# A fused attention, mixture and attention network: an earlier split of expert weights through PSUM, and loads in finer pieces

## The chip, the cores and the metric

One core of a Trainium2 chip runs the whole program. The metric is the device time of one execution in microseconds, the median of several; less is better. Times in the trace are microseconds from the first instruction.

The engines are TensorE (PE; PEld is its loading of weights), VectorE (DVE), ScalarE (ACT), GpSimd (POOL) and SyncE (SP). Each works its own list of instructions in order, and they wait for each other by semaphores.

## What is computed

Four layers on `x` of 8 x 512 tokens with 128 channels, each behind a layer norm and added to `x`: a recurrent attention, a mixture of 8 experts, a second recurrent attention with an MLP, and a mixture of 16 experts. The change lies at the end of the first layer and around the second:

```python
logits = jax.nn.relu(x @ rw1 + rb1) @ rw2 + rb2
vals, ids = jax.lax.top_k(logits, K)                    # K = 2 of E = 8
probs = jax.nn.softmax(vals, axis=-1)
...
pos = jnp.cumsum(m, axis=0) - 1                         # place of a token in its expert
keep = (pos_tok < CAP).astype(x.dtype)                  # CAP = 512
disp = jnp.zeros((E, CAP, Cx), x.dtype).at[ids_f, pos_c].add(xr * keep[:, None])
h = jax.nn.relu(jnp.einsum('enc,ech->enh', disp, ew1) + eb1[:, None, :])
eo = jnp.einsum('enh,ehc->enc', h, ew2) + eb2[:, None, :]
y = eo[ids_f, pos_c] * (probs_f * keep)[:, None]
return y.reshape(Bx, Tx, K, Cx).sum(axis=2)
```

## The kernel before

The program runs in stages, split by barriers: at `stage_end(eng, k)` an engine adds to `stage_done` and waits until all four compute engines have; GpSimd only adds to it, and SyncE takes no part. B = 8 batches of 512 tokens, each NT = 4 tiles of 128.

**Stage 5** ends the first attention and routes the tokens. It is one pipeline over the batches, written out by hand on each engine. In iteration b TensorE makes the router's hidden layer (`router_hidden`), the transposed logits (`router_logits_T`), the transposed tokens of the next batch (`transpose5`), the variance of the attention's output two batches on (`variance_o`, four matmuls with one column) and the logits by token (`router_logits`). ScalarE applies relu, copies the transposed tokens as float16 (`xT5_copy`) and takes square roots (`deviation_o` waits for the variance). VectorE makes the low half of the tokens (`xT5_low`, L1405), picks the two largest logits (`route`), turns counts into slots of `disp` (`place_picks`, whose last line L1438 signals `slots`), and adds the attention's output two batches on.

GpSimd copies rows of tokens to `disp` in DRAM: `scatter(b)` issues eight indirect DMAs (L635), one for each tile and choice, 64 in all. It waits for the slots of batch b, and at the third tile, ahead of the fifth DMA, for the logits of batch b + 1 (in the last batch for `s_eb2_mm`, the experts' output bias spread over the partitions by TensorE).

Products of 32-bit values are made of float16 halves: the high half of a value w is w * 1024 rounded to float16, the low half is what is left, and three matmuls (`PARTS`) replace one. For the 8 experts `weights0_high(k)` (ScalarE, L890) and `weights0_low(k)` (VectorE, L1472) make the halves of 1024 columns, k = 0 to 3 for the first layer and 4 to 7 for the second. Six of the eight are made at the end of stage 5, two inside stage 6. The float16 halves lie in A2 and A3, where the rows to be scattered lie before them, so the high halves wait for the scatters of batches 0 to 3 (`s_scattered[0]`) and 4 to 6 (`s_scattered[1]`).

At its end TensorE runs `unread` passes, matmuls of 512 columns whose result nobody reads, 20 ahead of the barrier and 18 behind it. VectorE copies the spread bias (`eb2_rep`, L1466), makes the low halves, and then the coefficients of the two experts from ScalarE's Exp (L1479 to L1483). SyncE waits until all scatters have landed and loads `disp` into `xd` by four DMAs of two experts each (L498).

**Stage 6** runs the experts: `transpose_rows(e)`, float16 halves on ScalarE (L904) and VectorE (L1489), `hidden0(e)` and `outputs0(e)` on TensorE. GpSimd scatters the outputs to `y_rows` in DRAM.

**Behind it** SyncE loads `y_rows` back, two DMAs of 256 KB for each batch (L507, one for each choice). `combine(b)` on VectorE (L1537) adds both choices to `resid` by eight multiply-adds, four for each choice, and then makes the statistics of the next layer norm. These loads lie in the same tiles (A6, A7) as the experts' weights before.

PSUM has 8 banks of 512 columns. In stage 5 banks 0 to 3 carry the attention's centred output, the transposed tokens and the router's hidden layer, bank 4 the projection, bank 5 the transposed logits, 6 the logits and counts, 7 the variances; 6 and 7 then the spread bias.

## Time and profile before

| | us |
|---|---|
| median of 3 runs | 928.3 (927.37 to 928.76) |
| the profiled execution | 927.65 |
| its span, first to last instruction | 925.6 |
| mean granted TensorE clock | 0.962 |

```profile
## 1 busy us (share of the span) xinstructions
PE 774.7 (84%) x6154; PEld 469.3 (51%) x6154; DVE 693.2 (75%) x2078; ACT 622.2 (67%) x932; POOL 632.3 (68%) x414
```

The 2.05 us between the span and the profiled execution's time lie outside the instructions. Stage 5 runs from about 208 to 323 us, the experts from 331 to 384, the return starts at 388. A record gives the start of an instruction, its duration, and in brackets how long its engine sat idle before it and what ended that. A row in which an operation carries xN merges N of them.

### The profile page before, as it was taken

The page shows a single profiled execution, that of the slowest core. Times are in us where ns is not written, and L with a number is a line of the kernel's source. Part 1 is how long each engine was busy: PE and PEld are TensorE (multiplying, and loading weights), DVE is VectorE, ACT ScalarE, POOL GpSimd, SP SyncE. Part 2 cuts the span into 40 slices and gives each one's busy share as a digit, 9 for nine tenths or more (in the row PEclk, how much of TensorE's full clock was granted, in tenths as well). Part 3 has the DMA queues.
Part 4 walks back from the last instruction along what each step waited for, and adds up shares of the span by engine and source line. Part 5 has one row for each costly group of instructions (what it writes and reads, how often), then busy time and mean ns, then how long its engine had stood idle before and what let it go on. Part 6 is the DMA issues. An engine that isn't in the chain of part 4 may idle for free.

```text
span 925.6 us, 18384 instructions
## 1 busy us (share of the span) xinstructions
PE 774.7 (84%) x6154; PEld 469.3 (51%) x6154; DVE 693.2 (75%) x2078; ACT 622.2 (67%) x932; POOL 632.3 (68%) x414
## 2 busy tenths in 40 slices
PE   4965765669998689468787989999999999999997
PEld 1343221224543357323233756767776777777775
DVE  7769899985777558498999878776666666666664
ACT  3755233323455367248778988888888888989895
POOL 4008899730577727558798997686868686868695
PEclk9987899899999899879999999999999999999999
DMA  5999300008200030252600000000000000000000
GB/s 150 118 120 202 115 0 0 18 3 211 69 21 7 3 101 26 68 149 58 204 1 1 1 1 2 13 1 11 0 11 0 8 4 0 11 0 11 0 13 13
DMA packets 52761, 40.47 MB, mean 44 GB/s; under 512 B 6028, under 2 KB 44703, under 8 KB 52703
## 3 DMA queue, kind: packets, MB, share of 16 engines
q1 hardware_dynamic: 49630, 37.28, 18.5%
q0 software_dynamic: 3072, 2.51, 0.9%
q8 instruction: 24, 0.39, 0.2%
q14 instruction: 35, 0.28, 0.1%
HBM read 18.07 MB, written 14.88 MB: 36 GB/s over the span
## 4 chain that ended last, share of the span: by engine, by line
POOL 24%; PE 18%; issue 14%; DVE 14%; ACT 6%; DMA 1%; POOLq 0%; DVEq 0%; ACTq 0%; SPq 0%
POOL scratch L725 20%; PE PS L1874 17%; DVE scratch L1635 2%; DVE resid L1537 2%; DVE stats L1375 1%; DVE scratch L1643 1%; POOL disp L635 1%; POOL resid L711 1%; PE PS L1881 1%; ACT scratch L1163 1%; ACT scratch L1159 1%; DVE resid L1388 1%; DVE A L1400 1%; DVE scratch L1378 1%; ACT A L1094 1%
## 5 line engine op out<-in xcount | busy, mean ns | idle before, releaser
L725 POOL TENSOR_TENSOR scratch<-scratch 128x1024 f16<-128x1024 f32 x128 | 273.0, 2135 | 84.5 <-ACT scratch L1163 82.3
L1822 DVE SCALAR_TENSOR_TENSOR resid<-PS,coef,resid 128x128 f32<-128x128 f32 x512 | 144.0, 344 | 108.8 <-PE PS L1874 103.4
L1874 PEld LDWEIGHTS PS<-A,scratch 128*128 128x128 f16 x3456 | 203.4, 98 | 37.9 <-POOL scratch L725 4.9
L1874 PE MATMUL PS<-A,scratch 128*128 128x128 f16 x3456 | 217.1, 219 | 3.9 <-POOL scratch L725 1.6
L1874 PE MATMUL PS<-A 128*128 (+1 forms) x768 | 186.8, 379 | 0.8 <-DVE A L1666 0.2
L1159 ACT ACTIVATE scratch<-PS,cols 128x512 f32<-128x512 f32 x256 | 163.9, 683 | 25.9 <-PE PS L1874 19.0
L1163 ACT ACTIVATE scratch<-scratch 128x1024 f16<-128x1024 f32 x128 | 135.3, 1057 | 5.0
L1874 PE MATMUL PS<-scratch,ident 128*128 128x512 f32 x160 | 89.4, 681 | 51.9 <-DVE scratch L1341 51.9
L594 POOL TENSOR_TENSOR scratch<-A 128x1024 f32<-128x1024 f32 x32 | 76.0, 2384 | 73.2 <-DVE A L1310 56.2
L1874 PEld LDWEIGHTS PS<-A 128*128 128x128 f16 x768 | 70.7, 98 | 66.6 <-issue 0.7
L635 POOL DMA_INDIRECT disp<-A,scratch x64 | 65.5, 1023 | 36.4 <-issue 30.0
L1874 PEld LDWEIGHTS PS<-scratch,ident 128*128 128x128 f32 x160 | 30.8, 210 | 100.0 <-DVE scratch L1341 77.7
L1332 DVE TENSOR_TENSOR_SCAN PS<-PS,scratch 128x512 f32<-128x512 f32 x64 | 74.9, 1216 | 1.9
L1874 PE MATMUL PS<-scratch,A 128*128 128x512 f16 (+1 forms) x216 | 52.5, 389 | 2.1 <-DVE scratch L1489 1.1
L652 POOL DMA_INDIRECT y_rows<-A x32 | 34.3, 1072 | 28.7 <-DVE A L1504 24.7
L1881 PE MATMUL PS<-ident,scratch 128*128 128x128 f32 x128 | 21.5, 294 | 36.7 <-ACT scratch L949 16.7
L674 POOL TENSOR_TENSOR scratch<-scratch,A 128x1024 f32<-128x1024 f32 x16 | 38.6, 2415 | 12.2 <-DVE scratch L1635 4.4
L1874 PE MATMUL PS<-scratch,w_r 128*8 128x512 f32 (+1 forms) x106 | 40.2, 509 | 5.9 <-DVE scratch L1718 3.0
L663 POOL TENSOR_SCALAR A<-resid,scratch 128x128 f32<-128x128 f32 x32 | 31.3, 988 | 19.6 <-DVE scratch L1549 19.6
L818 ACT ACTIVATE PS<-A 128x512 f32<-128x512 f32 x33 | 19.7, 599 | 35.8 <-DVE PS L1332 35.7
L818 ACT ACTIVATE PS<-scratch 128x512 f32<-128x512 f32 x31 | 18.6, 601 | 36.6 <-DVE PS L1332 36.0
L1635 DVE TENSOR_TENSOR_SCAN scratch<-PS,scratch 128x512 f32<-128x512 f32 x32 | 37.3, 1207 | 2.5 <-POOL scratch L674 1.2
(334 smaller groups left out, 1321.0 us busy)
## 6 DMA issues: line engine op xcount, KB each, us to landing
A<-A SPq DMA_DIRECT2D x22, 256.0 KB, 7.5
y_rows<-zeros SPq DMA_DIRECT2D x8, 512.0 KB, 6.0
A<-y_rows SPq DMA_DIRECT2D x16, 256.0 KB, 3.5
disp<-zeros SPq DMA_DIRECT2D x4, 528.0 KB, 21.6
A<-disp SPq DMA_DIRECT2D x4, 528.0 KB, 6.0
resid<-in_L_attn_x SPq DMA_DIRECT2D x8, 256.0 KB, 4.0
A<-scratch SPq DMA_DIRECT2D x8, 256.0 KB, 6.9
A<-in_L_ffn_ew SPq DMA_DIRECT2D x1, 2048.0 KB, 12.4
```

The costliest lines, as they stand in the source:

```text
L594: pool.tensor_tensor(c_ring[n % 3], bkR[:, 2 * p:2 * p + 2, :], vR[:, i, :].unsqueeze(1).to_broadcast([128, 2, T]), MUL).then_inc(S("r0_c" ...
L635: pool.indirect_dma_start(out=disp[:, :], in_=rows5[RING_OF[b]][:, k, t, :], in_offset=None, out_offset=bass.IndirectOffsetOnAxis(ap=slot_ ...
L652: pool.indirect_dma_start(out=y_rows[:, :], in_=eo[:, ex * NT + t, :], in_offset=None, out_offset=bass.IndirectOffsetOnAxis(ap=xd[:, ex * ...
L674: pool.tensor_tensor(cbuf[n % 2], cs[n % 2], v1[:, bts(b, T)].unsqueeze(1).to_broadcast([128, 2, T]), MUL).then_inc(S("r_c"), 1)
L725: pool.tensor_tensor(h_low[n % 4], h_full[n % 2], h_high[n % 4], SUB).then_inc(S("m1_low"), 1)
L818: A_(bank(n % 2), kk_pair(a, m)[:, max(i, j) % 2, :], ACT.Identity, scale=-1.0, bias=1.0).then_inc(S("r0_decay"), 1)
L1159: A_(h_full[e % 2][:, h * T:(h + 1) * T], bank((e * HC1 + h) % 4), ACT.Gelu, scale=1.0 / SCALE, bias=cols[:, MB1 + e * HC1 + h:MB1 + e * H ...
L1163: A_(h_high[e % 4], h_full[e % 2], ACT.Copy).then_inc(S("m1_high"), 1)
L1332: V.tensor_tensor_scan(out=bank(2 + 2 * (n % 2) + u), data0=bank(u), data1=c_ring[n % 3][:, u, :], initial=0.0, op0=MUL, op1=ADD).then_inc ...
L1635: last = V.tensor_tensor_scan(out=state[:, j, :], data0=bank(2 + j), data1=cbuf[n % 2][:, j, :], initial=0.0, op0=MUL, op1=ADD)
L1822: last = STT(out=resid[:, g, :], in0=bank(4 + e % 2)[:, t * C:(t + 1) * C], scalar=coef[b % 2][:, t, e:e + 1], in1=resid[:, g, :], op0=MUL ...
L1874: return nc.tensor.matmul(o, l, r, start=start, stop=stop)
```

## The change

Two changes are made together.

In stage 5 TensorE runs `variance_o(b + 2)` behind `router_logits(b)` and no longer ahead of it. GpSimd's wait for the logits of batch 1 moves from the third tile of batch 0 to the fourth. ScalarE makes the first three high halves at the ends of iterations 5, 6 and 7. It copies each of the first six high halves back, as 32-bit values, to PSUM (banks 0 and 1, or 2 and 3, in turn), and VectorE's low half reads it there. A copy waits for its own high half and, from the third on, for the low half two before it. Exp comes behind the third copy. VectorE copies `eb2_rep` behind the six low halves. The unread passes go to bank 4, 30 ahead of the barrier and 6 behind it.

The loads of `disp` are one expert, one expert, three and three. The return of batch 0 comes in halves of two tiles, four DMAs, counted by the semaphores of the `disp` loads; `combine(0)` works on each half when it is there. SyncE waits for landed loads from batch 3 on, no longer from batch 2.

On TensorE, from one iteration of stage 5 (transposes of the next batch, L1881 and L1916; logits, L2027 and L2062; `meancol` is the variance's operand), before:

```order
L1874 MATMUL PS<-scratch,w_r 8x512 x4
L1881 MATMUL PS<-ident,A 128x128 x4
L1874 MATMUL PS<-meancol,scratch 128x1 x4
L2027 MATMUL PS<-ident,scratch 128x8 x4
L1874 MATMUL PS<-w_q,scratch 128x128 x4
```

and now:

```order
L1909 MATMUL PS<-scratch,w_r 8x512 x4
L1916 MATMUL PS<-ident,A 128x128 x4
L2062 MATMUL PS<-ident,scratch 128x8 x4
L1909 MATMUL PS<-meancol,scratch 128x1 x4
L1909 MATMUL PS<-w_q,scratch 128x128 x4
```

The logits stand ahead of the variance; nothing else moved there. On ScalarE, from iteration 7 of stage 5 to the first expert (relu L857, logits L863, high halves L890, transposed rows L904), before:

```order
L857 ACTIVATE scratch<-PS,cols 128x512 x4
L863 ACTIVATE scratch<-PS 8x512
L893 ACT_TABLE_LOAD
L893 ACTIVATE tmpb<-tmpa 128x32
L890 ACTIVATE A<-A 128x2x512 x6
L904 ACTIVATE scratch<-PS 128x512 x2
```

and now, from the second early high half in the iteration before (L894 high halves, L901 copies to PSUM, L926 Exp):

```order
L894 ACTIVATE A<-A 128x2x512
L877 ACTIVATE scratch<-PS,cols 128x512 x4
L883 ACTIVATE scratch<-PS 8x512
L894 ACTIVATE A<-A 128x2x512
L901 ACTIVATE PS<-A 128x1024 x3
L926 ACT_TABLE_LOAD
L926 ACTIVATE tmpb<-tmpa 128x32
L894 ACTIVATE A<-A 128x2x512
L901 ACTIVATE PS<-A 128x1024
L894 ACTIVATE A<-A 128x2x512
L901 ACTIVATE PS<-A 128x1024
```

Two high halves moved into the rounds, the third ahead of Exp, six copies are new, and the table load stands behind three of them. On VectorE, behind the last batch's routing, before:

```order
L1464 TENSOR_TENSOR tmpa<-scratch 128x32
L1466 COPY A<-PS 128x1024
L1475 TENSOR_TENSOR w_r<-pickg 128x512
L1472 SCALAR_TENSOR_TENSOR A<-A 128x2x512 x6
L1479 TENSOR_SCALAR tmpa<-tmpb 128x32
```

and now:

```order
L1496 TENSOR_TENSOR tmpa<-scratch 128x32
L1504 TENSOR_TENSOR w_r<-pickg 128x512
L1501 SCALAR_TENSOR_TENSOR A<-A,PS 128x2x512 x6
L1508 COPY A<-PS 128x1024
L1510 TENSOR_SCALAR tmpa<-tmpb 128x32
```

The copy of the bias moved behind the low halves, which now read A and PSUM instead of A twice.

The diff:

```diff
--- before.py
+++ after.py
@@ -381,7 +381,20 @@
         e0_hl1 = A2[:, :].bitcast(f16).rearrange("p (e s n) -> p e s n", e=E0, s=2)
         e0_hl2 = A3[:, :].bitcast(f16).rearrange("p (e s n) -> p e s n", e=E0, s=2)
         E0_SPLITS = 2
+        EARLY, BESIDE = 3, 6
+
+        def high_made(k):
+            return at(E0_SPLITS + (k if k < EARLY else 2 * k if k < BESIDE else k + BESIDE))
+
+        def beside_made(k):
+            return at(E0_SPLITS + (EARLY + k if k < EARLY else 2 * k + 1))
+
+        def high_at(k):
+            return bank(k % 2 * 2, 2)
+
         PARTS = ((0, 0), (0, 1), (1, 0))
+        XD_PARTS = ((0, 1), (1, 2), (2, 5), (5, E0))
+        XD_PART_OF = (0, 1, 2, 2, 2, 3, 3, 3)
 
         r7 = carve(7)[:, 688:688 + 2 * TILES].rearrange("p (s n) -> p s n", s=2)
         nm7 = carve(7)[:, 752:752 + TILES]
@@ -494,15 +507,22 @@
             sp.wait_ge(s_scattered[1], 16 * TOP0 * NT * (B - 5))
             sp.wait_ge(s_scattered[2], 16 * TOP0 * NT)
             dv = disp.rearrange("(n p) c -> p n c", p=128)
-            for k in range(E0 // 2):
-                sp.dma_start(xd[:, bts(k, 2 * NT), :], dv[:, bts(k, 2 * NT), :]).then_inc(s_disp[k], 16)
+            for k, (low, high) in enumerate(XD_PARTS):
+                part = slice(low * NT, high * NT)
+                sp.dma_start(xd[:, part, :], dv[:, part, :]).then_inc(s_disp[k], 16)
 
             sp.wait_ge(s_eo, 16 * E0 * NT)
             sp.wait_ge(S("split_low"), at(E0_SPLITS + 7))
             yv = y_rows.rearrange("(k n p) c -> k p n c", k=TOP0, p=128)
             for b in range(B):
-                if b >= 2:
-                    sp.wait_ge(s_fetched[b % 2], X_LOADS + 16 * TOP0 * (b // 2))
+                if b == 0:
+                    for half in range(2):
+                        for k in range(TOP0):
+                            part = slice(half * NT // 2, (half + 1) * NT // 2)
+                            sp.dma_start(fetched[k][:, part, :], yv[k][:, part, :]).then_inc(s_disp[half], 16)
+                    continue
+                if b >= 3:
+                    sp.wait_ge(s_fetched[b % 2], X_LOADS + 16 * TOP0 * ((b - 1) // 2))
                 for k in range(TOP0):
                     sp.dma_start(fetched[k][:, bts(b, NT), :], yv[k][:, bts(b, NT), :]).then_inc(s_fetched[b % 2], 16)
 
@@ -626,9 +646,9 @@
                 pool.wait_ge(S("rows5"), at(b))
                 pool.wait_ge(S("ids5"), at(b))
                 for t in range(NT):
-                    if t == NT // 2 and b + 1 < B:
+                    if t == (NT // 2 if b else NT - 1) and b + 1 < B:
                         pool.wait_ge(S("lg5_mm"), at(b + 1))
-                    elif t == NT // 2:
+                    elif t == NT // 2 and b + 1 == B:
                         pool.wait_ge(s_eb2_mm, 1)
                     for k in range(TOP0):
                         g = b * NT + t
@@ -868,6 +888,18 @@
             deviation_x5(0)
             deviation_o(1)
             xT5_copy(0)
+            def weights0_high(k):
+                hl, w = ((e0_hl1, e0w1), (e0_hl2, e0w2.rearrange("p e i c -> p e (i c)")))[k // 4]
+                two = slice(2 * (k % 4), 2 * (k % 4) + 2)
+                A_(hl[:, two, 0, :], w[:, two, :], ACT.Copy, scale=SCALE).then_inc(S("split_high"), 1)
+
+            def weights0_beside(k):
+                hl = (e0_hl1, e0_hl2)[k // 4]
+                if k >= 2:
+                    act.wait_ge(S("split_low"), at(E0_SPLITS + k - 2))
+                act.wait_ge(S("split_high"), high_made(k))
+                A_(high_at(k), hl[:, 2 * (k % 4):2 * (k % 4) + 2, 0, :], ACT.Copy).then_inc(S("split_high"), 1)
+
             for b in range(B):
                 for h in range(HC0):
                     relu5(b, h)
@@ -884,18 +916,18 @@
                     square_o(2)
                 elif b + 2 < B:
                     deviation_o(b + 2)
-            def weights0_high(k):
-                hl, w = ((e0_hl1, e0w1), (e0_hl2, e0w2.rearrange("p e i c -> p e (i c)")))[k // 4]
-                two = slice(2 * (k % 4), 2 * (k % 4) + 2)
-                A_(hl[:, two, 0, :], w[:, two, :], ACT.Copy, scale=SCALE).then_inc(S("split_high"), 1)
-
+                if b >= B - EARLY:
+                    act.wait_ge(s_wm, 32)
+                    act.wait_ge(s_scattered[0], 16 * TOP0 * NT * 4)
+                    weights0_high(b - B + EARLY)
+            for k in range(EARLY):
+                weights0_beside(k)
             act.wait_ge(S("lg_less"), at(0))
             A_(tmpb[:, :], tmpa[:, :], ACT.Exp).then_inc(S("lg_exp"), 1)
-            act.wait_ge(s_wm, 32)
-            act.wait_ge(s_scattered[0], 16 * TOP0 * NT * 4)
             act.wait_ge(s_scattered[1], 16 * TOP0 * NT * (B - 5))
-            for k in range(6):
+            for k in range(EARLY, BESIDE):
                 weights0_high(k)
+                weights0_beside(k)
             stage_end(act, 5)
 
 
@@ -1462,19 +1494,18 @@
                 if b + 2 < B:
                     add_o(b + 2)
             TT(tmpa[:, :], top0[:, 1, :], top0[:, 0, :], SUB).then_inc(S("lg_less"), 1)
-            dve.wait_ge(s_eb2_mm, 1)
-            st.done(V.tensor_copy(eb2_rep, bank(6, 2).rearrange("p k (e c) -> p (k e) c", c=C)))
-
             def weights0_low(k):
                 hl, w = ((e0_hl1, e0w1), (e0_hl2, e0w2.rearrange("p e i c -> p e (i c)")))[k // 4]
                 two = slice(2 * (k % 4), 2 * (k % 4) + 2)
-                dve.wait_ge(S("split_high"), at(E0_SPLITS + k))
-                STT(out=hl[:, two, 1, :], in0=w[:, two, :], scalar=SCALE, in1=hl[:, two, 0, :],
+                dve.wait_ge(S("split_high"), beside_made(k) if k < BESIDE else high_made(k))
+                STT(out=hl[:, two, 1, :], in0=w[:, two, :], scalar=SCALE, in1=high_at(k) if k < BESIDE else hl[:, two, 0, :],
                     op0=MUL, op1=SUB).then_inc(S("split_low"), 1)
 
             TT(pick2, pickg[:, 0], pickg[:, 1], ADD)
-            for k in range(6):
+            for k in range(BESIDE):
                 weights0_low(k)
+            dve.wait_ge(s_eb2_mm, 1)
+            st.done(V.tensor_copy(eb2_rep, bank(6, 2).rearrange("p k (e c) -> p (k e) c", c=C)))
             dve.wait_ge(S("lg_exp"), at(0))
             st.done(TS(tmpa[:, :], tmpb[:, :], 1.0, None, ADD))
             st.done(V.reciprocal(tmpa[:, :], tmpa[:, :]))
@@ -1530,14 +1561,18 @@
 
 
             def combine(b):
-                dve.wait_ge(s_fetched[b % 2], X_LOADS + 16 * TOP0 * (b // 2 + 1))
-                for k in range(TOP0):
-                    for t in range(NT):
-                        g = b * NT + t
-                        last = STT(out=resid[:, g, :], in0=fetched[k][:, g, :], scalar=coef0[:, k, g:g + 1],
-                                   in1=resid[:, g, :], op0=MUL, op1=ADD)
-                    if k < TOP0 - 1:
-                        links.done(last)
+                if b:
+                    dve.wait_ge(s_fetched[b % 2], X_LOADS + 16 * TOP0 * ((b + 1) // 2))
+                for part in ((0, 1), (2, 3)) if b == 0 else (range(NT),):
+                    if b == 0:
+                        dve.wait_ge(s_disp[part[0] // 2], BACK[part[0] // 2] + 16 + 16 * TOP0)
+                    for k in range(TOP0):
+                        for t in part:
+                            g = b * NT + t
+                            last = STT(out=resid[:, g, :], in0=fetched[k][:, g, :], scalar=coef0[:, k, g:g + 1],
+                                       in1=resid[:, g, :], op0=MUL, op1=ADD)
+                        if k < TOP0 - 1:
+                            links.done(last)
                 last.then_inc(S("moe_added"), 1)
                 dve.wait_ge(S("moe_added"), at(b))
                 token_stats(b).then_inc(S("x_var"), 1)
@@ -1590,7 +1625,7 @@
                 dve.wait_ge(S("gate_high"), at(m))
                 TT(gate_hl[:, 1, c], whole_gate(m), gate_hl[:, 0, c], SUB).then_inc(S("gate_low"), 1)
 
-            dve.wait_ge(S("split_high"), at(E0_SPLITS + 8))
+            dve.wait_ge(S("split_high"), high_made(8))
             for low, w, high in ((u1_hl[:, 1, :], u_1[:, :], u1_hl[:, 0, :]), (u2_hl[1], u_2[:, :, :], u2_hl[0]),
                                  (ur_hl[:, 1, :], u_r[:, :], ur_hl[:, 0, :])):
                 STT(out=low, in0=w, scalar=SCALE, in1=high, op0=MUL, op1=SUB)
@@ -2052,9 +2087,9 @@
                 router_logits_T(b)
                 if b + 1 < B:
                     transpose5(b + 1)
+                router_logits(b)
                 if b and b + 2 < B:
                     variance_o(b + 2)
-                router_logits(b)
                 if b == 0:
                     centre(2)
                     unread(3, 4)
@@ -2067,13 +2102,13 @@
             for e in range(E0):
                 last = mm(tile(bank(6 + e // 4), e % 4), spread[:, e, :], eb2[:, :])
             last.then_inc(s_eb2_mm, 1)
-            unread(3, 20)
+            unread(4, 30)
             stage_end(pe, 5)
-            unread(3, 18)
+            unread(4, 6)
 
 
             def transpose_rows(e):
-                pe.wait_ge(s_disp[e // 2], BACK[e // 2] + 16)
+                pe.wait_ge(s_disp[XD_PART_OF[e]], BACK[XD_PART_OF[e]] + 16)
                 pe.wait_ge(S("xdT"), at(e, 2))
                 transposes(bank(e % 2), xd[:, bts(e, NT), 0:C]).then_inc(S("trd"), 1)
```

## Rows read from the trace of the kernel before

**Rows 1.** Chain of waits, 320 to 330 us: start, us, what.
```profile
323.24 2.11 DMA disp<-A,scratch
325.43 4.01 DMA A<-disp
```
**Rows 2.** GpSimd's timeline, stage 5: start, us, what, [idle before <-releaser].
```profile
244.04 0.97 POOL L635 DMA_INDIRECT disp<-A,scratch  x1 [3.93 <-PE PS L2027]
...
286.10 0.97 POOL L635 DMA_INDIRECT disp<-A,scratch  x1 [0.50 <-issue]
...
301.53 0.97 POOL L635 DMA_INDIRECT disp<-A,scratch  x1 [0.30 <-issue]
...
306.65 0.97 POOL L635 DMA_INDIRECT disp<-A,scratch  x1 [0.30 <-issue]
...
315.60 1.52 POOL L635 DMA_INDIRECT disp<-A,scratch  x1 [0.31 <-issue]
317.42 1.97 POOL L635 DMA_INDIRECT disp<-A,scratch  x1 [0.30 <-issue]
319.69 1.96 POOL L635 DMA_INDIRECT disp<-A,scratch  x1 [0.30 <-issue]
```
**Rows 3.** TensorE's timeline: variance, logits, unread passes, first expert.
```profile
284.02 0.95 PE L1874 MATMUL PS<-meancol,scratch 128*128 128x1 f32 x8
284.90 0.41 PE L2027 MATMUL PS<-ident,scratch 8*128 8x8 f32 x4
...
304.85 0.41 PE L2027 MATMUL PS<-ident,scratch 8*128 8x8 f32 x4 [0.68 <-ACT scratch L863]
...
313.35 5.81 PE L1874 MATMUL PS<-pickg,ones 128*128 128x512 f16 x20
323.07 5.64 PE L1874 MATMUL PS<-pickg,ones 128*128 128x512 f16 x18 [3.91 <-DVEq L181]
...
331.68 5.63 PE L1874 MATMUL PS<-scratch,A 128*128 128x512 f16 x24 [1.11 <-DVE scratch L1489]
```
**Rows 4.** VectorE's timeline, 299 to 323 us.
```profile
299.90 0.16 DVE L1438 TENSOR_TENSOR scratch<-scratch 128x8 int32<-128x8 f32 x1
...
309.44 0.18 DVE L1464 TENSOR_TENSOR tmpa<-scratch 128x32 f32<-128x32 f32 x1
313.45 1.22 DVE L1466 COPY A<-PS 128x1024 f32<-128x1024 f32 x1 [3.83 <-PE PS L1874]
...
315.05 6.89 DVE L1472 SCALAR_TENSOR_TENSOR A<-A 128x1024 f16<-128x1024 f32 x6
...
322.80 0.18 DVE L1483 TENSOR_TENSOR scratch<-scratch,tmpb 128x32 f32<-128x32 f32 x1
```
**Rows 5.** ScalarE's timeline, 297 to 319 us.
```profile
297.03 1.33 ACT L857 ACTIVATE scratch<-PS,cols 128x512 f32<-128x512 f32 x2 [1.18 <-PE PS L1874]
...
304.81 1.28 ACT L893 ACT_TABLE_LOAD   x1
...
313.23 5.79 ACT L890 ACTIVATE A<-A 128x1024 f16<-128x1024 f32 x6 [3.35 <-DMA disp<-A,scratch]
```
**Rows 6.** TensorE by windows: window, length, PE busy (count), clock, DMA share, GB/s.
```profile
323.00:324.00 1.00, 0.93 (x3) 0.50 0.02 1
...
406.00:408.00 2.00, 0.73 (x2) 1.00 0.56 162
```
**Rows 7.** The return: timelines of SyncE and VectorE, line L507, a smaller load.
```profile
388.47 16.12 SPq L507 DMA_DIRECT2D A<-y_rows  x16
...
392.40 2.31 DVE L1537 SCALAR_TENSOR_TENSOR resid<-A,scratch,resid 128x128 f32<-128x128 f32 x8 [8.18 <-DMA A<-y_rows]
...
L507 SPq DMA_DIRECT2D A<-y_rows x16: 359/508/515, 388.5 to 404.1; - x16
...
DMA to landing us min/median/max: 2.9/3.5/4.6
...
A<-scratch SPq DMA_DIRECT2D x32, 64.0 KB, 2.0
```

## What the change was predicted to do

> **What bounds the kernel now.** First the chain of waits over 300 to 340 us [rows 1]. The last of 64 scatters of tokens to `disp` starts at 323.24; 2.11 us later SyncE issues the loads of `disp` (325.43), the first lands 4.01 us later (329.44), and after transposes, ScalarE's high half and VectorE's low half TensorE starts on the experts' first matmuls at 331.68 [rows 3], 2.24 us behind the landing. From there TensorE is the bound of the mixture, so what is gained before it moves everything behind it. The barrier of the stage opens at 323.07 [rows 3], 6.4 us before the landing: it isn't late now.
>
> Second, GpSimd's timeline [rows 2]. The scatters go at one per 1.28 us (0.97 busy, 0.30 between). They wait once in each batch of eight for the router's logits of the next batch: with logits at 284.90 + 0.41 = 285.31 [rows 3] the scatter behind the wait starts at 286.10, 0.79 later, and that row has 0.50 idle instead of 0.30. So each wait costs 0.2 us, and 0.79 is the least distance between release and start. Then three scatters are stretched, to 1.52, 1.97 and 1.96 us. They lie inside the six low halves of the weights on VectorE, 315.05 to 321.94 [rows 4], whose two inputs are both in SBUF; the scatters beside VectorE's copy from PSUM at 313.45 and beside ScalarE's high halves [rows 5] keep their pace.
>
> Last, the return from the mixture [rows 7]: SyncE issues at 388.47, VectorE starts at 392.40 after 8.18 us idle and needs 2.31 for eight multiply-adds. Everything later waits for that.
>
> **The change part by part.**
>
> *The low halves read the high half from PSUM.* If the second SBUF input is what stretches the scatters, this gives back 0.55 + 1.00 + 0.99 = 2.54 us (1.52, 1.97, 1.96 against 0.97) [rows 2]. Nothing in the trace shows a scatter beside such an operation with one input in PSUM; the nearest row is the copy from PSUM at 313.45, which stretched none. Bounds 0 and 2.54, I take 2.54. The rule of the Trainium skill bears on it both ways (SBUF — State Buffer, "Who interferes with whom"): two SBUF inputs hold a port pair shared with GpSimd, one does not; but it adds, marked as inferred, that such an operation takes only the read side, while making descriptors needs the write side. By the first the sum keeps its 2.54, by the second the stretching had another cause and would stay, which is rival 1.
>
> *Variance behind the logits, and the first batch's wait moved by two scatters.* The four small matmuls of a variance take 0.88 us of TensorE ahead of the logits (284.02 to 284.90 [rows 3]); the logits come that much earlier in iterations 1 to 5. VectorE's routing doesn't start earlier, since it is still busy with the low half of the transposed tokens when the logits are there. GpSimd saves its 0.2 us a batch. In the first batch two more scatters go ahead of the wait of 3.93 us [rows 2]. Neither can bring more than the next limits allow: the scatters of a batch wait for its slots (batch 6: 299.90 + 0.16 = 300.06 [rows 4], first scatter 301.53, so 301.53 − 300.06 − 0.79 = 0.68 us of slack), and the logits of batch 7, which have no variance ahead of them, come at 304.85 + 0.41 = 305.26 against a scatter at 306.65: 306.65 − 305.26 − 0.79 = 0.60 us. So the scatters gain 0.60 (bounds 0.4 and 0.7). The variance's later reader on ScalarE slips 0.2 us and has over a microsecond of idle behind it.
>
> Together the last scatter and the load's issue move by 3.14: issue at 325.43 − 3.14 = 322.29.
>
> *Finer loads of `disp`.* Expert 0 alone is 264 KB. Loads of 256 KB land in 2.9 (shortest) to 3.5 us (median) [rows 7], two experts took 4.01. I take 3.2; expert 1, issued under 0.9 later, lands at about 4.0 as now, and its transposes (0.5) hide in the 2.24 us that expert 0 needs to its first matmul. First matmul by this path: 322.29 + 3.2 + 2.24 = 327.73, against 331.68: **3.95 us** earlier (3.1 if expert 0 lands no earlier than both now).
>
> *The barrier, which hid and may now bind.* ScalarE's first two early high halves (six in a row take 5.79, 0.97 each; one alone, whose end nothing hides, I take as 1.05) fit in idle time of its rounds, the tightest 1.18 us [rows 5]. After its last router copy (304.80): third high half to 305.8, copies to PSUM 0 and 1 to 307.8 (no row shows such a copy; 1024 columns from SBUF took 1.05, I take the same, bound 1.2). VectorE is through its routing at 309.62, `pick2` to 310.0, lows 0 and 1 at 1.15 each to 312.3; ScalarE's third copy waits for low 0 and ends at 312.3; then the table load for Exp, which now lies open (1.28), and Exp (0.23): 313.8. Then three times high half, wait for itself, copy: 1.08 + 0.97 = 2.05 each, the last copy ending at 320.1; low 5 to 321.35; `eb2_rep`, moved behind, 1.22; the five small operations that take 321.87 to 322.98 now, 1.11. Sum: barrier at about 323.75, 0.7 later than now. A matmul of 512 columns costs 0.235 us at the full clock (24 in 5.63 at 331.68 [rows 3]). The 20 unread passes from 313.35, 5.81 us, become 30, 5.81 + 10 × 0.235 = 8.16, to 321.5; TensorE is idle 2.2 us; six passes after the barrier take 1.4, to 325.15. Expert 0's rows land at 325.5. So the barrier is hidden by 0.3 us, and each further microsecond of it costs one. If ScalarE's copies take 1.2, it comes 0.5 later and costs 0.2.
>
> *The clock.* Granted clock was 0.50 of full (1.2 of 2.4 GHz) in 323 to 324, after 3.91 us idle, and stayed 1.00 in 406 to 408, with 0.73 of 2 us busy [rows 6]. Idle of 2.2 us lies between the two; I take it to stay up, with the other case as rival 2.
>
> *Return in halves.* A first half needs two loads of 128 KB. 64 KB landed in 2.0, 256 KB in 2.9 to 3.5 [rows 7]; I take 2.5. Issues cost 0.51 each: second load at 388.98, landed 391.5; four multiply-adds to 392.75; the second half, issued to 390.0, landed 392.5, done at 394.05 against 392.40 + 2.31 = 394.71: **0.65 us** (0 if 128 KB take as long as 256; 1.3 with 2.0). The loads of batch 1 are issued 1 us later but are needed at 397.
>
> *The rest.* Six more copies on ScalarE are counted above; the eighth and seventh weight splits keep both inputs in SBUF, inside the mixture, where TensorE binds. Different banks for the unread passes cost nothing.
>
> **Sum.** 3.95 + 0.65 = 4.6 us off the profiled execution of 927.65 gives 923.05; off the median of 928.3, 0.65 above it, **923.7**. What separates from no change is 0.2%, 1.86 us, so 926.44.
>
> **Rivals.**
>
> 1. *The scatters stay stretched* (the cause is not the second SBUF input). Three lows now end by 313.5 and three run from 316 to 321.4, beside the last scatters, so about the same 2.54 us are lost again. Issue 324.83, first matmul 330.27, gain 1.4 + 0.65 = 2.05: **926.2**. For: nothing shows the mixed form. Against: the stretch begins and ends with the lows.
>
> 2. *The barrier and the clock bind.* The clock falls in the idle time before the barrier: six passes at half of it, 0.47, take 2.8, transposes start at 326.55, and with the transposes' own slowness (0.4) the first matmul comes at 329.2. The 18 passes behind the barrier now took 5.64 us [rows 3] against 18 × 0.235 = 4.23: 1.4 us is what the lower clock costs until it rises, and that would fall on the experts' matmuls. Gain 331.68 − 329.2 − 1.4 = 1.1, plus 0.65: **926.5**. For: the drop after 3.91 us idle and only six passes instead of 18 behind the barrier. Against: the idle time is shorter by 1.7 us.
>
> 3. *Slower: the scatters, moved against VectorE's rounds by 0.6 us, hold up its SBUF-only operations.* A round is 10.5 us and VectorE's chain bounds it. If a scatter held up the chain by its own 0.97 us in each of seven rounds, that is 6.8 us, against 4.6 gained: **930.5**. It turns slower than no change beyond 0.66 us a round. Against: now scatters cover three quarters of each round, so most phases are tried already, and rounds don't vary.
>
> 4. *Finer loads bring nothing*, neither for `disp` nor in the return: 3.1 + 0 = 3.1: **925.2**, still faster.
>
> **How the numbers follow.** Forecast with its small variations (922.4 to 924.7) 0.56; rival 4 and cases between 0.10; rival 1 0.10, of which half below 926.44; rival 2 0.17, of which 0.06 faster; rival 3 0.05; other losses 0.02. Faster: 0.56 + 0.10 + 0.05 + 0.06 = 0.77. Same: 0.05 + 0.11 + 0.01 = 0.17. Slower: 0.05 + 0.01 = 0.06. The range reaches from 922.3 (both bounds of the small gains) to 926.9, past rivals 1 and 2; about 0.1 lies outside above and less below.
>
> **What would show it.** In the changed profile: all scatters from the 57th on at 0.97, else the first step is wrong; the last scatter starts near 320.1; the load of `disp` is issued near 322.3 and lands first near 325.5; the barrier opens near 323.75 (later than 324.2: my count of ScalarE's pairs is wrong, and TensorE's start is read from the barrier instead); the granted clock is 1.00 behind it; first expert matmul near 327.7; rounds still 10.5 us; 16 returns, then VectorE's eighth multiply-add of batch 0 ends 0.65 us sooner after SyncE's issue. From the first expert matmul to SyncE's return issue should stay 56.8 us; if not, something moved inside the mixture that I have not seen.

## The result and the profile after

| | before | after |
|---|---|---|
| median of 6 runs | 927.84 us (927.0 to 928.91) | 924.11 us (922.24 to 925.51) |
| profiled execution, its span | 927.65, 925.6 | 925.51, 923.3 |
| mean granted TensorE clock | 0.962 | 0.953 |

The ratio is 0.9958, 95% interval 0.9947 to 0.9968: 3.7 us faster, where 4.6 was forecast (923.7, range 922.3 to 926.9). The profiled execution was forecast at 923.05 and took 925.51.

The profiled execution after is the slowest of its six. Its stages 1 to 3, which the change doesn't touch, took 2.0 us longer, so absolute times of the two traces can't be set side by side. TensorE's granted clock was lower there: 0.77 against 0.89 over 45 to 75 us, 0.83 against 0.90 over 100 to 150 us. I count all times of stage 5 and of the experts from the first unread pass of stage 5: 208.33 before, 210.35 after. "At 112.21" below means 112.21 us after that pass.

| us after the first unread pass of stage 5 | before | after | forecast gain | gain |
|---|---|---|---|---|
| last scatter starts | 114.91 | 112.21 | 3.14 | 2.70 |
| SyncE issues the loads of `disp` | 117.10 | 114.39 | 3.14 | 2.71 |
| first rows landed, behind the issue | 4.01 | 2.98 | 0.8 | 1.03 |
| first expert matmul | 123.35 | 119.61 | 3.95 | 3.74 |
| from there to the issue of the return | 56.79 | 56.75 | 0 | 0.04 |
| from that issue to batch 0's last multiply-add | 6.24 | 5.55 | 0.65 | 0.69 |

(The third row is a duration from the issue in the row above it; the last two are durations too.)

The chain of waits of the kernel after (start, us, what) against [rows 1]:

```profile
322.56 2.11 DMA disp<-A,scratch
324.74 2.98 DMA A<-disp
...
327.76 0.67 PE PS L1916 x4
```

GpSimd's timeline after, against [rows 2]. The scatters from the 57th on (at 313.62) all take 0.97. The waits in the middle of the batches have not gone: GpSimd sits idle 0.62 to 0.69 us there in batches 1 to 5, where it was 0.50 or less before, and only in batch 6 (308.49) nothing more than the usual 0.30:

```profile
287.63 0.97 POOL L655 DMA_INDIRECT disp<-A,scratch  x1 [0.69 <-issue]
...
298.27 0.97 POOL L655 DMA_INDIRECT disp<-A,scratch  x1 [0.62 <-issue]
...
308.49 0.97 POOL L655 DMA_INDIRECT disp<-A,scratch  x1 [0.31 <-issue]
...
317.45 0.97 POOL L655 DMA_INDIRECT disp<-A,scratch  x1 [0.31 <-issue]
318.72 0.97 POOL L655 DMA_INDIRECT disp<-A,scratch  x1 [0.30 <-issue]
320.00 0.97 POOL L655 DMA_INDIRECT disp<-A,scratch  x1 [0.30 <-issue]
```

TensorE after, against [rows 3]: logits of batch 7, 30 passes, then the barrier (2.29 idle), six passes, and the transposes right behind them, released by the rows' landing with 0.20 idle:

```profile
307.30 0.41 PE L2062 MATMUL PS<-ident,scratch 8*128 8x8 f32 x4 [0.68 <-ACT scratch L883]
...
315.86 7.94 PE L1909 MATMUL PS<-pickg,ones 128*128 128x512 f16 x30
326.08 1.47 PE L1909 MATMUL PS<-pickg,ones 128*128 128x512 f16 x6 [2.29 <-DVEq L181]
327.76 0.66 PE L1916 MATMUL PS<-ident,A 128*128 128x128 f32 x4 [0.20 <-DMA A<-disp]
...
329.96 5.63 PE L1909 MATMUL PS<-scratch,A 128*128 128x512 f16 x24 [0.67 <-DVE scratch L1520]
```

VectorE after, against [rows 4]: low halves waiting for ScalarE's copies, the bias copy behind them, the last coefficient 0.09 us ahead of the barrier's opening:

```profile
312.39 3.52 DVE L1501 SCALAR_TENSOR_TENSOR A<-A,PS 128x1024 f16<-128x1024 f32 x3
318.30 1.22 DVE L1501 SCALAR_TENSOR_TENSOR A<-A,PS 128x1024 f16<-128x1024 f32 x1 [2.38 <-ACT PS L901]
320.39 1.22 DVE L1501 SCALAR_TENSOR_TENSOR A<-A,PS 128x1024 f16<-128x1024 f32 x1 [0.88 <-ACT PS L901]
322.49 1.22 DVE L1501 SCALAR_TENSOR_TENSOR A<-A,PS 128x1024 f16<-128x1024 f32 x1 [0.88 <-ACT PS L901]
323.63 1.22 DVE L1508 COPY A<-PS 128x1024 f32<-128x1024 f32 x1
...
325.81 0.18 DVE L1514 TENSOR_TENSOR scratch<-scratch,tmpb 128x32 f32<-128x32 f32 x1
```

The return after (VectorE), against [rows 7]: two groups of four multiply-adds. SyncE's first issue is at 386.71.

```profile
389.44 1.26 DVE L1572 SCALAR_TENSOR_TENSOR resid<-A,scratch,resid 128x128 f32<-128x128 f32 x4 [6.98 <-DMA A<-y_rows]
391.00 1.26 DVE L1572 SCALAR_TENSOR_TENSOR resid<-A,scratch,resid 128x128 f32<-128x128 f32 x4 [0.30 <-DMA A<-y_rows]
```

### The profile page after: what moved, and what is told of

The parts are those of the page before. It is cut to its first block, busy times and chain, and to the rows that moved or that the text cites. A ratio compares the mean times of both kernels' runs of the same rounds, so it can differ in the third digit from the quotient of the medians.

```text
span 923.3 us, 18395 instructions
## 1 busy us (share of the span) xinstructions
PE 779.5 (84%) x6152; PEld 471.9 (51%) x6152; DVE 693.6 (75%) x2078; ACT 628.5 (68%) x938; POOL 628.3 (68%) x414
## 4 chain that ended last, share of the span: by engine, by line
POOL 24%; PE 19%; DVE 14%; issue 14%; ACT 6%; DMA 1%; POOLq 0%; SPq 0%; DVEq 0%; ACTq 0%
POOL scratch L745 21%; PE PS L1909 18%; DVE scratch L1670 2%; DVE resid L1572 2%; DVE stats L1407 1%; DVE scratch L1678 1%; POOL resid L731 1%; PE PS L1916 1%; DVE resid L1420 1%; ACT scratch L1195 1%; ACT scratch L1191 1%; DVE A L1432 1%; DVE scratch L1410 1%; ACT A L1126 1%; POOL scratch L694 1%
## 5 line engine op out<-in xcount | busy, mean ns | idle before, releaser
L655 POOL DMA_INDIRECT disp<-A,scratch x64 | 62.5, 977 | 36.9 <-issue 32.7
L1916 PE MATMUL PS<-ident,scratch 128*128 128x128 f32 x128 | 21.5, 295 | 36.2 <-ACT scratch L981 16.0
```

What stands on the lines that cost most here:

```text
L655: pool.indirect_dma_start(out=disp[:, :], in_=rows5[RING_OF[b]][:, k, t, :], in_offset=None, out_offset=bass.IndirectOffsetOnAxis(ap=slot_ ...
```

## Experiments

All are variants of the changed kernel. The ratios are to the kernel before on the same chip: it took 927.84 us beside the changed kernel, 927.46 beside e1 to e4, and 928.74 beside e7, e5b, e6b and e8b. So small differences between medians of different sets are better read from the ratios. The last two columns are from one trace each, in us after the first unread pass of stage 5.

| kernel | median us | ratio, 95% interval | last scatter | first expert matmul |
|---|---|---|---|---|
| changed | 924.11 | 0.9958 (0.9947 to 0.9968) | 112.21 | 119.61 |
| e1_low_from_sbuf | 927.54 | 0.9999 (0.9989 to 1.0010) | 115.85 | 123.21 |
| e2_no_early | 930.60 | 1.0037 (1.0025 to 1.0050) | 112.25 | 126.27 |
| e3_disp_by_two | 924.91 | 0.9968 (0.9957 to 0.9980) | 112.26 | 120.72 |
| e4_return_whole | 923.74 | 0.9963 (0.9949 to 0.9977) | 112.28 | 119.62 |
| e7_passes_18 | 927.37 | 0.9988 (0.9977 to 0.9999) | 112.23 | 121.80 |
| e5b_order_back | 924.20 | 0.9956 (0.9939 to 0.9974) | 112.36 | 119.68 |
| e6b_variance_back | 923.08 | 0.9945 (0.9925 to 0.9965) | 112.41 | 119.60 |
| e8b_tail_behind | 923.94 | 0.9946 (0.9929 to 0.9963) | 112.35 | 119.83 |

### The second SBUF input

```diff
-STT(out=hl[:, two, 1, :], in0=w[:, two, :], scalar=SCALE, in1=high_at(k) if k < BESIDE else hl[:, two, 0, :],
+STT(out=hl[:, two, 1, :], in0=w[:, two, :], scalar=SCALE, in1=hl[:, two, 0, :],
```

> The changed kernel, but the low halves read the high half from SBUF again, as before; ScalarE still makes the copies to PSUM, and VectorE still waits for them, so nothing but the place of one input differs. Times are counted from the first unread pass of stage 5, where before and after start alike: the last scatter starts at 114.91 us before the change and at 112.21 behind it. Theory (the second SBUF input stretches the scatters): scatters beside the six low halves last 1.5 to 2.0 instead of 0.97, the last one starts 2 to 5 us later than 112.21, the experts' first matmul (119.61 behind the change) follows it, and the median is 2 to 4 us above the changed kernel's 924.1. Rival (the stretching came from something else, such as the traffic of that moment or the descriptors' writing): the scatters keep 0.97 and the time stays within 1 us of the changed kernel's.

GpSimd's timeline of e1_low_from_sbuf:

```profile
313.67 1.97 POOL L655 DMA_INDIRECT disp<-A,scratch  x1 [0.30 <-issue]
315.94 0.97 POOL L655 DMA_INDIRECT disp<-A,scratch  x1 [0.30 <-issue]
317.22 0.97 POOL L655 DMA_INDIRECT disp<-A,scratch  x1 [0.30 <-issue]
318.50 1.94 POOL L655 DMA_INDIRECT disp<-A,scratch  x1 [0.30 <-issue]
320.74 1.79 POOL L655 DMA_INDIRECT disp<-A,scratch  x1 [0.30 <-issue]
322.83 1.79 POOL L655 DMA_INDIRECT disp<-A,scratch  x1 [0.30 <-issue]
324.92 0.97 POOL L655 DMA_INDIRECT disp<-A,scratch  x1 [0.30 <-issue]
```

and VectorE's, its low halves:

```profile
312.44 3.53 DVE L1501 SCALAR_TENSOR_TENSOR A<-A 128x1024 f16<-128x1024 f32 x3
318.36 1.23 DVE L1501 SCALAR_TENSOR_TENSOR A<-A 128x1024 f16<-128x1024 f32 x1 [2.38 <-ACT PS L901]
320.45 1.23 DVE L1501 SCALAR_TENSOR_TENSOR A<-A 128x1024 f16<-128x1024 f32 x1 [0.87 <-ACT PS L901]
322.55 1.22 DVE L1501 SCALAR_TENSOR_TENSOR A<-A 128x1024 f16<-128x1024 f32 x1 [0.87 <-ACT PS L901]
```

Only the place of one input differs, and four scatters are stretched again: 1.97, 1.94, 1.79 and 1.79, together 3.6 us, as much as the last scatter comes later (115.85 against 112.21). The last three long ones each lie across one low half (318.36, 320.45, 322.55), and the two scatters in VectorE's pause between 315.97 and 318.36 keep 0.97. The low half itself takes 1.22 us either way. The rival is refuted, and the time is back at that of the kernel before. Of the rules of the Trainium skill that the prediction weighed (SBUF — State Buffer, "Who interferes with whom"), the first, that two SBUF inputs contend with GpSimd and one does not, agrees with this trace (1.79 to 1.97 us here beside two inputs in SBUF, 0.97 in the changed kernel beside one); the remark marked there as inferred, which would have spared the scatters, does not. Which step inside a scatter is held up no run shows.

This experiment shows a second thing. TensorE is idle 2.23 us before the barrier, makes its six passes in 1.47, waits 3.64 us for the rows, and the granted clock falls afterwards. TensorE's timeline and windows (length, busy and count, clock, DMA share, GB/s) of e1_low_from_sbuf:

```profile
331.26 0.66 PE L1916 MATMUL PS<-ident,A 128*128 128x128 f32 x4 [3.64 <-DMA A<-disp]
...
333.56 6.45 PE L1909 MATMUL PS<-scratch,A 128*128 128x512 f16 x24
```
```profile
328.00:331.00 3.00, 0.00 (x0) 1.00 0.48 129
331.00:334.00 3.00, 2.00 (x10) 0.73 1.01 256
334.00:337.00 3.00, 3.00 (x11) 0.70 1.09 300
```

The first 24 matmuls take 6.45 instead of 5.63 us, and the experts as a whole 57.41 instead of 56.75.

### The early high halves and the barrier

```diff
-        EARLY, BESIDE = 3, 6
+        EARLY, BESIDE = 0, 6
...
+            act.wait_ge(s_wm, 32)
+            act.wait_ge(s_scattered[0], 16 * TOP0 * NT * 4)
```

> The changed kernel with no early high halves: all six high halves and all six copies to PSUM come behind the scatters of batch 6, as the high halves did before. Theory (the barrier is bound by ScalarE's pairs at 2.05 us each and VectorE's tail of 2.3 us behind the last low half): six pairs take 12.3 us from about 315.0 on the clock of the changed kernel's profile, the barrier opens near 330.8 instead of 326.08, the experts' first matmul comes 4 to 5 us later than 119.61 us after the first unread pass of stage 5, and the median is near 928.5, no better than the kernel before. Rival (the barrier has slack, the loads of disp bind): the first matmul moves by less than 1 us and the median stays near 924.

TensorE's timeline of e2_no_early:

```profile
329.62 2.74 PE L1911 MATMUL PS<-pickg,ones 128*128 128x512 f16 x6 [6.13 <-DVEq L181]
332.16 1.65 PE L1918 MATMUL PS<-ident,A 128*128 128x128 f32 x8
334.76 1.47 PE L1911 MATMUL PS<-scratch,A 128*128 128x512 f16 x6 [0.96 <-DVE scratch L1522]
```

The barrier opens at 121.13 instead of 115.73 (5.40 later, 4.7 expected), the six passes take 2.74 instead of 1.47, with a granted clock of 0.50, that is 1.2 of 2.4 GHz, over 329 to 333 us, and the first matmul comes 6.66 later (126.27). The median is 930.6, 6.5 above the changed kernel and 3.1 above the kernel before. The mechanism is the expected one; its size was missed by some 2 us. 0.7 of it is the barrier's own delay, 1.27 the six passes at the lower clock, which I had not charged; from their end to the first matmul it takes 2.40 us against 2.41, so the transposes add nothing more. Reading from PSUM without the early high halves is thus slower than the kernel before.

### The pieces of the loads

```diff
-        XD_PARTS = ((0, 1), (1, 2), (2, 5), (5, E0))
-        XD_PART_OF = (0, 1, 2, 2, 2, 3, 3, 3)
+        XD_PARTS = ((0, 2), (2, 4), (4, 6), (6, E0))
+        XD_PART_OF = (0, 0, 1, 1, 2, 2, 3, 3)
```

> The changed kernel with the loads of disp two experts each again. Theory (finer loads give the difference between 4.0 us for two experts and 3.0 for one): the first landing is 4.0 us behind SyncE's issue instead of 2.98, the experts' first matmul comes 0.8 to 1.0 us later than 119.61, the median is 925.0. Rival (the second expert's rows, not the first's, release the first matmul, so that the finer loads bring nothing): no change within 0.2 us.

The chain of waits of e3_disp_by_two:

```profile
322.75 2.11 DMA disp<-A,scratch
324.93 4.03 DMA A<-disp
329.01 0.67 PE PS L1916 x4
```

4.03 us to the first landing against 2.98, and the first matmul at 120.72, 1.11 later than 119.61. The second expert's rows do not bind in the changed kernel: its transposes start at 118.28, 1.3 us ahead of the first matmul. The median is 0.8 us higher and the ratios are 0.9968 and 0.9958; their intervals overlap. The gain is shown by the trace, not by the medians.

### The return in halves

```diff
-                    for half in range(2):
-                        for k in range(TOP0):
-                            part = slice(half * NT // 2, (half + 1) * NT // 2)
-                            sp.dma_start(fetched[k][:, part, :], yv[k][:, part, :]).then_inc(s_disp[half], 16)
+                    for k in range(TOP0):
+                        sp.dma_start(fetched[k][:, 0:NT, :], yv[k][:, 0:NT, :]).then_inc(s_disp[0], 16)
...
-                for part in ((0, 1), (2, 3)) if b == 0 else (range(NT),):
+                for part in (range(NT),):
```

> The changed kernel with batch 0 returned in two whole loads and combined at once, as before; the looser waits of the later batches stay. Theory: from SyncE's first issue of the return to the end of batch 0's eighth multiply-add it takes 6.24 us again instead of 5.55, and the median is 0.7 us above the changed kernel's 924.1, 924.8. Rival (part of the 0.69 us is chance of one execution or due to the looser waits): the stretch stays under 5.9 us.

SyncE's and VectorE's timelines of e4_return_whole:

```profile
385.29 0.91 SPq L520 DMA_DIRECT2D A<-y_rows  x2
```
```profile
389.00 2.31 DVE L1570 SCALAR_TENSOR_TENSOR resid<-A,scratch,resid 128x128 f32<-128x128 f32 x8 [7.96 <-DMA A<-y_rows]
```

From issue to the end of the eighth multiply-add: 3.71 + 2.31 = 6.02 us. With halves it was 5.55 in the changed kernel's profile and between 5.0 and 5.6 in those of e1, e2, e3, e5b, e6b, e7 and e8b, which return in halves too. So by these traces halves are worth 0.4 to 1.0 us, and some 0.2 of the difference to 6.24 before is chance or the looser waits of the later batches. The measured 6.02 lies between what theory (6.24) and rival (under 5.9) expected. It is one trace against eight, and a first run of e8 (below), with halves, took 5.86; so the size stays rough. The medians of e4 and the changed kernel (923.74 and 924.11) don't show it: it is smaller than their intervals.

### The passes behind the barrier

```diff
-            unread(4, 6)
+            unread(4, 18)
```

> The changed kernel with 18 unread passes behind the barrier, as before the change, instead of 6; nothing else differs. Theory (once the loads land early, passes behind the barrier stand in the way of the transposes): passes start 115.73 us after the first unread pass of stage 5 and take 4.2 to 4.6 us, the transposes start near 120.1 instead of 117.41, the experts' first matmul comes 2.5 us later than 119.61, the median is 2.5 us above the changed kernel's. Rival (the barrier or the loads bind, passes are free): less than 0.5 us.

TensorE's timeline of e7_passes_18:

```profile
324.26 4.06 PE L1909 MATMUL PS<-pickg,ones 128*128 128x512 f16 x18 [1.06 <-DVEq L181]
328.16 1.04 PE L1916 MATMUL PS<-ident,A 128*128 128x128 f32 x8
330.30 4.06 PE L1909 MATMUL PS<-scratch,A 128*128 128x512 f16 x18 [1.11 <-DVE scratch L1520]
```

The passes end at 119.8, the transposes start at 119.66, 2.25 later than in the changed kernel, and the first matmul comes at 121.80, 2.19 later (2.5 expected). Passes that hid behind the loads before [rows 3] are in the way once the loads land early. The median is 3.3 us above the changed kernel's (2.8 by the ratios), of which the trace explains 2.2; the rest stays open.

### The order of stage 5

```diff
-                    if t == (NT // 2 if b else NT - 1) and b + 1 < B:
+                    if t == NT // 2 and b + 1 < B:
...
-                router_logits(b)
                 if b and b + 2 < B:
                     variance_o(b + 2)
+                router_logits(b)
```

e6 has the second edit alone. Both were run first on a chip on which the kernel before took 951.0 us; they were run again on another.

> The changed kernel with the variance ahead of the logits again and the first batch's wait at the third tile: the order of stage 5 is that of before. In the changed kernel the rounds lost 0.43 us in sum, VectorE's four normalising operations taking 1.15 to 1.22 instead of 1.12 in several rounds. Theory (the scatters, moved earlier, now overlap these operations and hold them up; the scatters gained 0.60 from earlier releases and lost 0.43 by the longer rounds): these operations take 1.12 again, rounds are 10.51 us, and the last scatter comes 0.17 us later than 112.21, the median within 0.3 of the changed kernel's. Rival (the longer rounds come from the new ScalarE work in iterations 5 and 6 or from nothing in the order): rounds stay longer and the last scatter comes 0.6 later.

> The changed kernel with only the variance ahead of the logits again; the first batch still has two more scatters ahead of its wait. Theory (the earlier logits are what lets the scatters run ahead in every round, the moved wait only helps in the first batch): scatters start ahead by 0.7 us in batch 1 and lose it again by about 0.2 us a round, the waits of 0.5 us come back, the last scatter is where the order of before puts it, 0.2 later than 112.21 at most. Rival (the moved wait carries the gain): the last scatter stays at 112.2 or earlier, with the normalising operations at 1.12.

> The changed kernel again, unchanged, to see on one chip beside the three other variants how much of its time varies from one execution to the next. Its profiled execution was its slowest of six (922.24 to 925.51), and in it stages 1 to 3, which the change leaves alone, took 2.0 us longer than in the profile before. Theory (those 2 us are chance of the early stages): another profile has the first unread pass of stage 5 between 208 and 211 us, and the stretch from there to the experts' first matmul again at 119.6 us within 0.2. Rival (the change itself shifts the early stages, through the code's place or its timing): the pass comes at 210.3 again, within 0.3.

> The changed kernel with VectorE's tail of stage 5, the copy of the spread bias and the five operations for the coefficients, behind the barrier, and 14 unread passes behind it instead of 6. It tries whether the barrier still binds anything. In the changed kernel the barrier opened at 326.08, the six passes ended at 327.55 and the first expert's rows had landed at 327.71, so both are tied. Theory (the loads bind by 0.2 us): the barrier opens 2.3 us earlier, the transposes start when the rows land as now, the first matmul moves by less than 0.2 us, and the median stays within 0.3 us of the changed kernel's. Rival (the barrier binds in executions whose loads are quick, or the experts' first steps on VectorE are delayed by the moved work): the median moves by more than 0.5 us, down in the first case, up in the second.

On the first chip the changed kernel took 944.8 us (ratio 0.9950, 0.9922 to 0.9978), e5 945.5 (0.9949), e6 944.7 (0.9933), e8 950.5 (0.9991, 0.9963 to 1.0019, single runs from 944.3 to 954.9). Small differences can't be read there: engines stood still for microseconds in stage 5 and inside the mixture. ScalarE's timeline of after_again, where a relu follows 3.94 us of idle time whose end the profile puts to no engine of the core:

```profile
299.82 1.27 ACT L877 ACTIVATE scratch<-PS,cols 128x512 f32<-128x512 f32 x2 [3.94 <-remote]
```

What it was I can't say. The run did answer its question: the first unread pass came at 208.26 where the same kernel had 210.35, so the 2 us of the early stages are chance, not the change. The lower clock alone doesn't make them: this trace too has 0.77 over 45 to 75 us. The stretch to the first matmul could not be compared.

Second run of the two orders:

> The same kernel as e5_order_back, once more, because its chip held up stage 5 of every kernel by 14 to 18 us and hid differences below one microsecond: variance ahead of the logits again, and the first batch's wait at the third tile. Theory: the normalising operations take 1.12 us again, rounds are 10.51, and the last scatter starts about 0.2 later than in the changed kernel (112.2 to 112.3 us after the first unread pass of stage 5). Rival: rounds stay longer and the last scatter comes 0.6 later.

> The same kernel as e6_variance_back, once more, for the same reason: only the variance ahead of the logits again. Theory (the logits' place lets the scatters run ahead in every round): waits of 0.5 us come back in the later batches and the last scatter starts 0.1 to 0.2 later than in the changed kernel. Rival (the moved wait in the first batch carries the gain): the last scatter stays at 112.2 or comes earlier.

VectorE's normalising operations of one round in the changed kernel, and the scatter that starts among them:

```profile
252.92 1.20 DVE L1432 TENSOR_SCALAR A<-resid,scratch 128x128 f32<-128x128 f32 x4
```
```profile
253.03 0.97 POOL L655 DMA_INDIRECT disp<-A,scratch  x1 [0.30 <-issue]
```

The same in e5b_order_back, and GpSimd's middle wait there, which has its 0.50 again:

```profile
251.04 1.12 DVE L1432 TENSOR_SCALAR A<-resid,scratch 128x128 f32<-128x128 f32 x4
```
```profile
251.94 1.07 POOL L655 DMA_INDIRECT disp<-A,scratch  x1 [0.30 <-issue]
...
286.31 0.97 POOL L655 DMA_INDIRECT disp<-A,scratch  x1 [0.50 <-issue]
```

Over the six rounds from batch 2 on the four operations take 1.19, 1.20, 1.15, 1.15, 1.22 and 1.24 us in the changed kernel, 1.11 or 1.12 in each round of e5b, and 1.20 once, in the second round, in e6b. What differs is where the scatters start, not whether one lies beside. With the old order, in e5b as in the kernel before, one scatter starts 0.38 or 0.39 us ahead of the four operations and one 0.89 or 0.90 behind their start, in each of four rounds (in the last 0.3 ahead and 0.97 behind); VectorE keeps its 1.12, and the second scatter takes 1.07 instead of 0.97. In the changed kernel a scatter starts 0.10 to 0.15 us behind their start, it keeps 0.97 in all but the last round (1.03), and VectorE's operations take up to 1.24. The size varies for reasons no run shows: in the first of these rounds they took 1.12 in e6b and 1.13 in e8b beside such a scatter.

With the old order the last scatter comes 0.15 later than in the changed kernel, with the variance alone moved back 0.20 later. But the other kernels with the new order (e2, e3, e4, e7, e8b) have it at 112.23 to 112.35, against 112.36 and 112.41, so the order is worth some 0.15 us at most and perhaps next to nothing. The expected mechanism holds: earlier releases move the scatters ahead, the scatters then start inside operations of VectorE, and the rounds grow by 0.43 in sum, which takes away most of the 0.60. The moved wait alone (e6b) brings nothing at the last scatter: its lead is gone when the middle waits catch up. By their medians none of these orders differs from the changed kernel.

### The barrier against the loads

```diff
             for k in range(BESIDE):
                 weights0_low(k)
+            stage_end(dve, 5)
             dve.wait_ge(s_eb2_mm, 1)
...
             TT(coef0[:, 1, :], keep[:, 1, :], tmpb[:, :], MUL)
-            stage_end(dve, 5)
...
-            unread(4, 6)
+            unread(4, 14)
```

> The same kernel as e8_tail_behind, once more, for the same reason: VectorE's tail of stage 5 behind the barrier, 14 unread passes behind it. Theory (loads and barrier are tied): barrier near 113.5 instead of 115.7, transposes when the first expert has landed (2.9 to 3.0 us behind SyncE's issue at 114.4), first matmul within 0.2 us of 119.6, median within 0.5 us of the changed kernel's. Rival: the first matmul moves by more than 0.5 us.

TensorE's timeline of e8b_tail_behind (the window shows 36 of its 44 passes): no idle time at the barrier any more, and the transposes wait for the rows.

```profile
317.83 8.19 PE L1909 MATMUL PS<-pickg,ones 128*128 128x512 f16 x36
326.72 0.66 PE L1916 MATMUL PS<-ident,A 128*128 128x128 f32 x4 [0.70 <-DMA A<-disp]
```

VectorE goes on behind the barrier at 113.78, where TensorE's six passes start at 115.73 in the changed kernel. The first matmul is at 119.83 against 119.61, the median 923.94. The barrier is 2 us earlier and brings nothing: the loads bind. In the changed kernel the passes behind the barrier end 0.17 us before the rows land, and twelve more of them cost 2.2 us (e7). So barrier and loads are tied there, and the next gain would need both.

## Why the prediction was right

**The scatters.** The 2.54 us for the PSUM input came as forecast: the 57th and later scatters take 0.97, and 2.70 − 2.54 = 0.16 is left for the order. e1 shows the cause. In the new arrangement the second SBUF input costs 3.6 us, more than the 2.54 of before, since four scatters meet a low half there and three did before.

**The order, mis-sized.** The term of 0.60 us measured some 0.15 at most. The limits were taken with the slots and the logits of batch 7 where they stood before: the logits came 307.30 − 2.02 = 305.28 against 304.85, 0.43 later. Their distance to the scatter behind them was the expected one (307.71 to 308.49, 0.78), and so it was one batch earlier (297.49 to 298.27). Nor did GpSimd save its 0.2 us a batch: eight scatters take 10.2 us and a round 10.5 or more, so over the rounds it waits in any case, and only where in a round its scatters lie can change. The rest is rival 3 in small: moved scatters hold up VectorE's normalising operations. I had priced it at up to 0.97 us a round and given it as a case of its own; it came at 0.03 to 0.12 us a round on the four operations, and should have been a term of the sum. The argument against it, that scatters cover three quarters of a round and so most phases are tried already, was wrong: in four rounds in a row the trace of before has them at one and the same place beside these operations (0.39 ahead and 0.89 behind their start).

**Finer loads.** 2.98 us to the first landing where I took 3.2, so this term gave 1.03 instead of 0.8. It made up for half of what the order fell short, which is luck; the second expert's rows came in time. e3: 1.1 us.

**The barrier.** Forecast 323.75 on the time scale of before, that is at 115.42; it opened at 115.73, 0.31 later, which the rounds' 0.43 covers: with the order of before (e5b) it opened at 115.24. ScalarE's copies to PSUM took 1.02 us each (1.05 taken) and the pairs 2.09 (2.05). The end of the six passes and the landing were 0.17 us apart, about as tight as worked out (0.3), so it was luck as much as reckoning that the barrier didn't bind.

**The clock.** The granted clock was 1.00 over 324 to 330 us, behind 2.29 us of idle time (TensorE's six passes took 1.47). It is lower behind the 6.13 us of e2, where the passes took nearly twice as long, and behind the 3.64 of e1; there only six passes lie between 2.23 and 3.64 us of idle time, so the 3.64 alone is not shown to be the cause. Rival 2 was a real mechanism, then. That 2.29 us would keep the clock could not be known from the rows of before, so taking it was a guess that came out; no trace has an idle time between 2.29 and 3.64 us at this place.

**The return.** 0.69 against 0.65; e4 gives 0.5 for the halves against the changed kernel's own trace. Traces with halves differ among themselves by 0.6 us and more, so the match to 0.04 is luck. The prediction counted 16 returns; with batch 0 in four there are 18.

**The sum.** The traces give 3.74 + 0.69 = 4.43 us, and 4.32 from the first unread pass of stage 5 to the end (717.27 and 712.95); the medians give 3.73. The remaining 0.6 to 0.7 is within what the rest of the program varies by: the first unread pass of stage 5 came between 208.3 and 210.5 us in the traces of kernels that are the same up to there, and the stretch from the issue of the return to the end took 535.4 to 537.1 us in the traces of this study. Which part of it falls on this comparison stays open.

## What to carry to other kernels

Where GpSimd issues indirect DMAs back to back on the critical path, look for VectorE operations with both inputs in SBUF beside them. Reading one input from PSUM kept VectorE's time here (1.22 us) and freed the DMAs (e1), but the engine that writes the copy must have room ahead of the barrier, or the gain turns into a loss (e2). Fillers that keep TensorE's clock up belong to the wait they fill, and have to be counted anew whenever that wait shrinks (e7) or grows (e1). A release that comes earlier in a pipeline of several engines is worth less than its distance to the next limit, since the limit moves too.

## What the runs showed of the hardware that was not expected

- VectorE's scalar operations with one SBUF input (L1432, four of them in 1.12 us) take up to 1.24 when a scatter starts 0.10 to 0.15 us behind their start: here it is VectorE that is held up, by some 0.1 us. When the scatter starts 0.89 us behind their start (before, e5b), it is the scatter that takes 0.1 us more (1.07).
- A scatter that meets a low half was stretched to at most 1.97 us, less than its own 0.97 and a whole low half of 1.22 together. In e1 the last three long ones start while 1.09, 0.94 and 0.94 us of the low half are left and grow by 0.97, 0.82 and 0.82, each 0.12 less: as if a scatter waited out what is left of the operation but for a first 0.12 us. That is an estimate from these rows.
- In one set of runs the kernel before took 951.0 us on its chip, in the other two sets 927.5 and 928.7. Of the changed kernel's 24 us there, 18.8 lie between stage 5's first pass and the first expert matmul and 7.5 in the mixture, less 2 in the early stages; the stretch behind the return was the same to 0.1 us (536.59 us).
